# Summing half of the power tables by accumulating transfers, and turning the first batch's rows on TensorE

## The reference

```python
h = tok(x, log_dt, log_w_real, w_imag)      # (8, 256, 512)
#   dt = exp(log_dt); w = -exp(log_w_real) + i*w_imag; dtA = w*dt       (256, 64)
#   Cm = Cc * (exp(dtA) - 1) / w;  K = einsum('chn,hnl->chl', Cm, exp(dtA * arange(512)));  h = 2*K.real
h = concatenate([h, txt], axis=1)           # (8, 384, 512)
h = h + attn(layernorm(h))                  # compress to 64, layernorm, q/k/v, rope, causal softmax, out
h = h + ffn(layernorm(h))                   # shared expert + top 2 of 8 routed experts, hidden 352
```

## Time and profile before

| | |
|---|---|
| median of 3 runs | 830.52 us |
| profiled execution, its own time | 835.92 us |
| its span, first to last instruction | 834.1 us |
| TensorE busy | 758.9 us, 91% |
| VectorE, ScalarE, GpSimd busy | 489.1, 310.3, 346.4 us |
| mean granted TensorE clock | 0.973 |

### The profile page before, as it was taken

The page is one execution under the profiler, slowest core; times in us unless marked ns, Lnnn a source line. Parts: engine busy times, 40 slices in busy tenths (PEclk is TensorE's granted clock), DMA queues, the critical chain, the costliest instruction groups (busy, mean ns, idle before and its releaser), DMA issues.

```text
span 834.1 us, 19002 instructions
## 1 busy us (share of the span) xinstructions
PE 758.9 (91%) x6723; PEld 474.8 (57%) x6724; DVE 489.1 (59%) x922; ACT 310.3 (37%) x600; POOL 346.4 (42%) x362
## 2 busy tenths in 40 slices
PE   0099998989889999999999989999999999999985
PEld 0099996645455454564555535656656565666652
DVE  7987658387884766657954524554444444444442
ACT  6767425144224261544423403333232322323221
POOL 2278651151480030400067743545455554455433
PEclk9999997679999999999999999999999999999998
DMA  5342171035345051777353457978768777676753
GB/s 219 71 134 80 42 248 52 22 101 127 70 137 103 27 153 53 186 204 171 97 140 86 129 119 180 174 136 137 149 121 139 132 136 137 133 143 123 122 98 52
DMA packets 127534, 101.84 MB, mean 122 GB/s; under 512 B 96016, under 2 KB 96144, under 8 KB 126960
## 3 DMA queue, kind: packets, MB, share of 16 engines
q1 hardware_dynamic: 99984, 45.74, 23.8%
q0 software_dynamic: 14240, 30.06, 19.9%
q10 hardware_dynamic: 13248, 25.17, 10.8%
HBM read 48.46 MB, written 28.15 MB: 92 GB/s over the span
## 4 chain that ended last, share of the span: by engine, by line
PE 75%; DVE 9%; DMA 6%; POOL 4%; issue 3%; ACT 2%; SPq 0%; POOLq 0%; DVEq 0%; ACTq 0%
PE PS L2213 11%; PE PS L2215 11%; PE PS L2214 11%; PE PS L1159 9%; PE PS L1160 9%; PE PS L1161 9%; PE PS L662 6%; PE PS L819 3%; DMA out_dram<-work 2%; PE PS L2236 2%; PE PS L1376 1%; DVE big L1519 1%; DVE work L1524 1%; POOL big L482 1%; DMA big<-x_dram,work 1%
## 5 line engine op out<-in xcount | busy, mean ns | idle before, releaser
L2213 PE MATMUL PS<-big,work 128*128 x493 | 165.8, 336 | 5.0 <-DMA work<-big 2.7
L2214 PE MATMUL PS<-big,work 128*128 x493 | 165.7, 336 | 0.0
L2215 PE MATMUL PS<-big,work 128*128 x493 | 165.7, 336 | 0.0
L2385 POOL DMA_INDIRECT out_dram<-work x55 | 88.1, 1602 | 115.5 <-DMA out_dram<-work 62.3
L2278 ACT ACTIVATE work<-PS 128x768 f16<-128x768 f16 x55 | 44.6, 810 | 163.9 <-PE PS L2236 163.9
L2327 DVE SCALAR_TENSOR_TENSOR work<-work 128x352 f16<-128x352 f32 x55 | 32.2, 586 | 89.6 <-ACT work L2285 89.6
L1768 POOL DMA_INDIRECT slots_dram<-work x48 | 48.9, 1019 | 79.8 <-DVE work L2129 61.4
L2369 POOL DMA_INDIRECT big<-x_dram,work x55 | 55.3, 1005 | 46.3 <-POOL work L2366 46.3
L2213 PEld LDWEIGHTS PS<-big,work 128*128 128x128 f16 x493 | 48.5, 98 | 39.8 <-issue 6.2
L2215 PEld LDWEIGHTS PS<-big,work 128*128 128x128 f16 x493 | 48.4, 98 | 36.3
L2214 PEld LDWEIGHTS PS<-big,work 128*128 128x128 f16 x493 | 48.4, 98 | 33.6
(11 more groups left out here) (282 smaller groups left out, 1628.1 us busy)
## 6 DMA issues: line engine op xcount, KB each, us to landing
big<-in_weights ACTq DMA_DIRECT2D x33, 272.0 KB, 3.9
work<-in_weights ACTq DMA_DIRECT2D x31, 272.0 KB, 3.1
work<-in_shared ACTq DMA_DIRECT2D x28, 256.0 KB, 3.2
x_dram<-big SPq DMA_DIRECT2D x24, 256.0 KB, 2.3
out_dram<-big SPq DMA_DIRECT2D x24, 256.0 KB, 2.4
big<-big SPq DMA_DIRECT2D x4, 384.0 KB, 4.7
big<-in_par SPq DMA_DIRECT2D x1, 1185.0 KB, 10.5
big<-in_c_real SPq DMA_DIRECT2D x1, 1024.0 KB, 5.6
```

The costliest lines, as they stand in the source:

```text
L2213: pe.matmul(out, x_high, w_high, start=start, stop=False)
L2214: pe.matmul(out, x_high, w_low, start=False, stop=False)
L2215: return pe.matmul(out, x_low, w_high, start=False, stop=stop)
L2385: pool.indirect_dma_start(out_d, bass.IndirectOffsetOnAxis(ap=S_NUM[u][:, 0:1], axis=0), YO[u], None, compute_op=ALU.add).then_inc(s_add[u ...
```

## The change

In the token stage the b half of chunks 1 to 7 gets its power tables PB1 and PB2 in three rotating buffers; DVE builds both, and a transfer issued by POOL adds PB2 to PB1 in SBUF. TensorE then runs two products instead of four in that half. The a half keeps four products, its P2 built by POOL (by DVE in chunk 1). The first five weight pieces for the norms come by one transfer at the start. In the attention part the third compression is split in three, the fourth comes ahead of `q_tensor(1)`, and the three row tiles of batch 0 are turned by TensorE from XS in SBUF, their remainders taken by DVE; the scores of pair 1 move behind the first FFN unit. The DRAM store of these rows stays, their turned load goes. `bias(1)` moves to the front of POOL's list, splits of the pieces 2 to 10 move to other places, and ACT runs one small Exp ahead of `copy_compressed(0)`.

```diff
+        def summed(n):
+            return 16 * (n // 3 + (n % 3 > 0))
 # tok_sync
+            sp.dma_start(NORM_IN..., a["shared"][:, 0:EARLY_NORMS * SP_COLS]).then_inc(s_norms, 16)
 # tok_scalar, tables(n): waits for G1_{n-2}b; wi for every chunk (b half only from chunk 2), im with both groups from chunk 2
+            act.wait_ge(s_norms, 16)
+            for q in range(3):
+                square_norm(act, q)
             tables(0)
...
-                for q in range(2 * n, min(2 * n + 2, MCH)):
-                    square_norm(act, q)
+                    if x == 0 and EARLY_NORMS + n < MCH:
+                        square_norm(act, EARLY_NORMS + n)
 # tok_gpsimd
+            def sum_b(n):
+                pool.wait_ge(tok_v.sem, tok_v.at(f"P2_{n}b"))
+                pool.dma_start(PB1[n % 3], PB2[n % 3], accum_op=ALU.add).then_inc(s_sum[n % 3], 16)
+            g2(0, "a")
+            g2(0, "b")
+            for n in CHUNKS[1:]:
+                if n not in VECTOR_P2:          # VECTOR_P2 = (1,)
+                    p2(n)                       # a half; waits im_n and mm{n-2}a
+                g2(n, "a")
+                if n >= 4:
+                    sum_b(n)
+                g2(n, "b")
+                if n < 4:
+                    sum_b(n)
 # tok_vector
+            def powers_b(n):
+                if n >= 3:
+                    dve.wait_ge(tok_p.sem, tok_p.at(f"mm{n - 3}b"))
+                p1(n, "b", grid(PB1[n % 3]))
+                p2(n, "b", grid(PB2[n % 3]))
+            for k in "ab":
+                p1(0, k, ...); p2(0, k, ...); g1(0, k)
+            powers_b(1)
+            for n in CHUNKS[1:]:
+                if n >= 2:
+                    dve.wait_ge(tok_p.sem, tok_p.at(f"mm{n - 2}a"))
+                p1(n, "a", ...)
+                if n in VECTOR_P2:
+                    p2(n, "a", ...)
+                g1(n, "a")
+                if n + 1 < NCHUNK:
+                    powers_b(n + 1)
+                g1(n, "b")
 # tok_tensor
+                    if n and x:
+                        pe.wait_ge(s_sum[n % 3], summed(n))
+                    products = [(power, coeff[u][...]) for power in (powers_of[:1] if n and x else powers_of) for coeff in (G1, G2)]
 # new functions of the attention part
+        def first_low(dve, t):
+            dve.wait_ge(lg_high, t + 1)
+            nc.vector.tensor_tensor(XS[t][:, D:2 * D], RX[t], XS[t][:, 0:D], ALU.subtract).then_inc(lg_low, 1)
+        def first_turn(pe):                     # 24 f16 transposes into banks 4, 5, 6
+            for part in range(2):
+                for t in range(3):
+                    if part == 0:
+                        pe.wait_ge(cm_a.sem, cm_a.at(f"cn{2 if t < 2 else 3}"))
+                    pe.wait_ge((lg_high, lg_low)[part], t + 1)
+                    for c in range(KC): mm = pe.transpose(...)
+        def first_columns(act): ...             # ACT copies t0 whole and the high half of t2 to XT_SH[0]
+        def first_rows(dve): ...                # DVE copies t1 whole and the low half of t2
 # attn_tensor
-            turn_probs(pe, 0, 0)
-            out_weights(pe)
-            turn_probs(pe, 0, 1)
             pe.wait_ge(tr_v.sem, tr_v.at(f"bank{2 * B - 4}"))
             pe.wait_ge(tr_a.sem, tr_a.at(f"bank{2 * B - 3}"))
-            compress(pe, 2)
+            compress(pe, 2, (0,))
+            turn_probs(pe, 0, 0)
+            turn_probs(pe, 0, 1)
+            out_weights(pe)
             values_tensor(pe, 0)
-            out_tensor(pe, 0)
-            q_tensor(pe, 1)
+            compress(pe, 2, (1,))
+            out_tensor(pe, 0, (0, 1))
+            compress(pe, 2, (2,))
+            out_tensor(pe, 0, (2,))
             compress(pe, 3)
+            q_tensor(pe, 1)
+            first_turn(pe)
             qkv_tensor(pe, 1)
-            scores_tensor(pe, 1)
-            pe.wait_ge(s_xt[0], 3 * 16)
+            turned_in(pe, 0)
             logits(pe, 0, XT_SH[0])
-            ffn_tensor(pe, 0, 4)
+            ffn_tensor(pe, 0, 1)
+            scores_tensor(pe, 1)
+            ffn_tensor(pe, 1, 4)
 # attn_vector (from the outputs of pair 0 on)
             scale_c(dve, 1, 1, 2)
+            out_stats(dve, 0, 0)
+            out_stats(dve, 0, 1)
             for w in OUT_ORDER[4:6]:
                 out_add(dve, 0, w)
+            out_stats(dve, 0, 2)
             moments(dve, 0, "a")
+            split_low(dve, 8)
+            norm_row(dve, 0); norm_row(dve, 1); first_low(dve, 0)
+            norm_row(dve, 2); first_low(dve, 1); first_low(dve, 2)
             for w in range(3, 6):
                 out_stats(dve, 0, w)
             moments(dve, 0, "b")
+            first_rows(dve)
+            rope_vector(dve, 1)
 # attn_gpsimd
+            bias(pool, 1)
             c_scale(pool, 1, 1, 2)
 # attn_scalar
+            act.activation(RSUM[:, 0, 0:1], lc("ones")[:, 0:1], ACT.Exp)
             copy_compressed(act, 0)
...
             exp_scalar(act, 0)
+            probs_scalar(act, 0, 0)
             copy_turned(act, 15)
             probs_scalar(act, 0, 1)
+            splits(act, 7, 8)                   # its load_piece(10) waits for split_low(6)
             ... WO copy
 # attn_sync
             store_rows(0)
-            sp.wait_ge(cm_p.sem, cm_p.at(f"c{PAIRS - 1}"))
-            load_turned(0)
```

More of the change, by code:

```diff
@@ L230, in build @@
         assert Q == HC * PW
+        HQ, PB_AT = Q // 2, 528
+        PB1, PB2 = ([x[u][:, HQ:Q] for u in range(2)] + [cut(work, PB_AT + k * HQ, HQ)] for k, x in enumerate((P1, P2)))
+        EARLY_NORMS = 5
+        NORM_IN = cut(big, Q, EARLY_NORMS, SP_COLS)
+        assert EARLY_NORMS * SP_COLS <= 2 * Q
         s_early, s_dt, s_w, s_c, s_late, s_par, s_rope, s_gate = (
@@ L389, in tables @@
                     act.wait_ge(set_v.sem, set_v.at("mag"))
[L390 to L394, removed]
+                at = 0 if n == 0 or n in VECTOR_P2 else HC * 4
+                for half in range(2):
+                    last = act.activation(bank(WI_BANK[n % 2], half, 1)[:, :, at:], turned(ROT, n, 1, 1, 2)[:, :, at:], ACT.Copy, scale=(1.0, -1.0)[half])
+                last.then_inc(tok_t.now(f"wi_{n}"), 1)
+                groups = 1 if n == 0 or n in VECTOR_P2 else 2
                 for half in range(2):
                     last = act.activation(turned(IM_ZW, n, half, 0, groups), turned(ROT, n, 1, 0, groups), ACT.Copy, scale=(1.0, -1.0)[half])
-                last.then_inc(tok_t.now(("zi" if n % 2 == 0 else "im") + f"_{n}"), 1)
+                last.then_inc(tok_t.now(f"im_{n}"), 1)
+            act.wait_ge(s_norms, 16)
+            for q in range(3):
+                square_norm(act, q)
             act.wait_ge(set_v.sem, set_v.at("mag_first"))
@@ L467, in tok_gpsimd, with part @@
                 pool.tensor_tensor(b1, b1, MAG_B[:, :, h0:h1].rearrange("p a h -> p h a"), ALU.mult).then_inc(set_g.now("mag2" + "ab"[x]), 1)
-            for n in CHUNKS:
-                u = n % 2
-                if n >= 2:
[L471 to L481, removed]
-                    pool.tensor_tensor(grid(G2[u])[:, h0:h1], slow(V, n, h0, h1), fast(ZI, n, h0, h1), ALU.mult).then_inc(tok_g.now(f"G2_{n}{k}"), 1)
+            def part(x, n, k):
+                return grid(x[n % 2])[:, HALVES[k]]
@@ L1743, in attn_gpsimd @@
                     deviation(pool, i, "ab"[half])
-                    rows_low(pool, 6 * i + 3 * half)
-                    if i == 0 and half == 0:
-                        bias(pool, 1)
+                    if i or half:
+                        rows_low(pool, 6 * i + 3 * half)
                     if i == 1 and half == 1:
@@ L1823, in attn_scalar @@
             copy_turned(act, 7)
[L1824 removed]
+            splits(act, 5, 6)
             v_scalar(act, 0)
```

225 lines of the change are left out of this document (139 added, 86 removed).

## The result

The changed kernel takes 818.78 us against 830.52 for the kernel before, medians of five runs each; the ratio, estimated from the runs and not from the two medians, is 0.9877, 95% interval 0.9833 to 0.992. The forecast was 808 in a range of 798 to 825: the sign is right, the gain is about half of what was forecast. A further measurement of the same kernel, six runs against 23 of before, gave 818.43 against 827.53, ratio 0.9866 (0.9808 to 0.9923).

A forecast was written before the change was run, and what follows sets the result against it. TensorE was taken to bound the kernel from 240 us on, unchanged, with gains only ahead of that: token stage -10.3, scores to logits -17.0, later waits +5, sum -22.3 us; 808 us against the median 830.52, range 798 to 825.

The forecast's parts named there:

- 17.0 us: Scores of pair 0 to first logits and half a unit beyond: gain of 17.0 us, bounds 20 and 7.
- Token stage, -10.3 forecast: Token stage: fewer TensorE products, POOL slowest at 6.5 us a chunk, end at 98.1 instead of 108.4 us.
- rival C: Token stage: the 3 us pause for sum 3 brings the clock down until compression 1 ends; 837 us, chance 0.07.
- Rival B: Token stage: sum slow to land or issue, TensorE waits in every b part; 816 to 818, up to 828; chance 0.15.
- From token stage to logits, 51.4 forecast: End of token stage to first logits: 51 us instead of 69.5, with no window at half clock.
- the split of piece 7 ahead of WO costs nothing: Before the WO copy: outputs free at 142.4 us, TensorE comes at 143.0, so the moved split costs nothing.
- I charge nothing: POOL's bias of pair 1, moved to DVE's statistics (136 to 144 us): no cost, 2.5 us at the upper bound.
- rival A: Second stretch, before the logits: the clock falls again, price 0.48 x 20.9 = 10 us; 818 us, chance 0.15.
- q, k, v as what is late next: Ahead of the first logits: q, k, v run until about 159.8 us, after the turned rows are copied by 159.3.
- A wait of 1.8 us ahead of unit 3: First FFN units: unit 3 needs the bank of unit 0, whose Silu is late on ACT; new wait of 1.8 us.
- The +5 for 200 to 240 us: After the logits: TensorE meets DVE's unchanged chores sooner and waits about 5 us more, bounds 0 and 10.
- rival D: Before 240 us: DVE and ACT absorb the second stretch's gain, 12 us lost; 820 us, chance 0.07.

The follow-up runs named there:

- the quick execution: One execution of the kernel before, unchanged, the same as h2; 826.85 us, nearest to the median.
- f4: The whole change with each sum issued as two transfers of half the columns; 817.03 us, ratio 0.9894 to the kernel before.
- f3: The whole change with a plain copy of PB2 over PB1 instead of the accumulating transfer; 816.45 us, ratio 0.9875 to the kernel before.
- the filled kernels: The kernel before with idle products in TensorE's two pauses of over 2.5 us: 20 and 18 of them, 828.4 us; 11 in each, 827.45 us.
- forecast's: The profiled execution of the kernel before, unchanged, from which the prediction was read; 835.92 us.
- f1: The kernel before, unchanged, executed once more for a second profile; 832.54 us.
- h2: The kernel before, unchanged, one execution; 826.85 us.
- h3: The kernel before, unchanged, one more execution; 828.78 us.

## Why the prediction was wrong in size

The step that failed is the last one, 808 = 830.52 - 22.3: it takes from the median a gain that was read from an execution which the median is not like. Two terms were too large besides. By its own steps, against the quick execution at the first FFN sum: -22.3 forecast, + 8.0 (clock) + 4.1 (token stage, 10.3 less 6.2) + 4.4 (to the logits, 69.5 less 51.4 forecast and 68.9 less 55.2 measured) - 2.7 (behind the logits, +6.1 forecast, +3.4 measured) = -8.5, as measured there.

- **The frame: the step that failed, 8.0 us.** To subtract from the median what the profile would gain holds only if the profile is like the median in the stage that changes. The text knew 5.4 us between the two and took the gain from the stretch where they were. Of its 17.0 us, 8.0 were recovered clock that an execution near the median had never lost (178.0 against 170.0). Profile against profile the change does show 17.2 of the 22.3 us.
- **Token stage, -10.3 forecast, -6.2 measured.** The landing (6.0 forecast, 5.1 to 6.9 with a median of 5.6), the issue (0.8; records of 0.85 to 1.77, but the next operation starts 0.6 later) and POOL's halves (1.9) were right. The pause of 3 us for sum 3 was 0.6, so rival C, the slower side, had no ground; where such a pause did come, 3.54 us in f4, the half clock behind it lasted 6.8 us and not 37. Wrong was what else those transfers touch: TensorE's instruction loads, 4.9 us of "issue" and then one short stretch at half clock, as far as the dates tell. The prediction had no term for it. Rival B looked for a late landing or issue; the sum is neither. The row that was set against 3.2 us for a plain copy, 4.1 for 256 KB, is of a transfer to DRAM; plain copies in SBUF took 3.4 in f3. (The prediction's dates have 86.3 where 67.0 and three times 6.5 give 86.5, which changes nothing.)
- **From token stage to logits, 51.4 forecast, 55.2 measured.** The forecast counts from the end of TensorE's last half chunk; counted from the copy's end, as the 55.2 are, it is 50.8. f4, whose clock stays up, needs 52.9, 2.1 more, of which the wait for the WO copy can explain 1.8; the other 2.3 us, up to 55.2, come with the clock. That the split of piece 7 ahead of WO costs nothing failed together with "I charge nothing" for the bias: neither brings the wait without the other. The rows showed the contention for tables of 384 columns, and it was looked for at the remainders, which ran undisturbed; it struck at operations of 6 columns, at 0.65 to 0.84 us more each, where DVE's split, ACT's load and the WO copy hang on one another. The fall of the clock behind it is rival A at a third of its price (0.48 x 6.8 us, 3.3), in this execution. The Trainium skill (SBUF — State Buffer, Who interferes with whom) has a VectorE instruction with two SBUF inputs contend with a GpSimd one that reads SBUF; these rows agree, 0.80 to 1.01 us beside POOL's bias and 0.15 to 0.17 without it.
- **q, k, v as what is late next** was right: with the wait taken off, the rows' chain (1.41 us) and q, k, v bound it at 52.7, within 1.9 us of the 50.8.
- **A wait of 1.8 us ahead of unit 3**: 2.08 measured. **The +5 for 200 to 240 us** was too much: from the logits to the first FFN sum the change is 3.4 us slower, and about 4 are the moved scores and this wait, already in the 17.0. What the 5 stood for, DVE holding TensorE up, is there on both sides: 2.62 us of wait at the sums of pair 1 in the quick execution, 2.81 in the change. Where it grows, in the filled kernels, it is rival D in small.
- **No change behind that point**: 607.9 against 608.2 us, right.

The chances gave 0.86 to faster, and faster it was. The value, 818.8, lies in the range and on the 818 of rivals A and B, each of which had 0.15, but that is luck: what happened is a piece of A, a cost beside B, and the frame, which no rival named.

None of the variants is shown to be faster than the whole change: even without the transfers the median is 816.2. What a cheaper sum would bring stays open. With the plain copy Y is complete 6 us earlier, the medians differ by 2 us, and the interval of its four runs is 6 us to either side.

## What to carry to other kernels

Before a forecast is set against the median, compare the profile's mean clock with that of the other runs: where a stage holds a stretch at half clock and the profile is one of the long executions, price that stage a second time at full clock. The sums here cost more than their landing (0.6 us of waiting for them, 4.9 of "issue"): ask what else the DMA engines carry at that time, the engines' instructions included. And when an operation is costed at nothing because another is short, check that other for a neighbour that may stretch it.

## What the hardware showed beyond that

- The same pause of 2.61 us, behind the same instructions, was followed by a granted clock of 0.50 for 23.9, 17.1, 3.4 and 3.4 us in four executions of one kernel (forecast's, f1, h2, h3). What decides between them stays open; the price was up to 9 us of 830. The wait of 1.8 us in the changed kernels varies likewise: 6.8 us at 0.50 right behind it, or none.
- An accumulating transfer of 512 KB in SBUF lands in 5.6 us (5.1 to 6.9) where a plain one takes 3.4 (2.9 to 4.9). The Trainium skill (DMA: Bandwidth & Descriptors, Anatomy of one DMA — SWDGE (gpsimd) path) fits one transfer by 2.0 us and 436 GB/s, 3.2 us for 512 KB, and doesn't say for which kind: the plain copies agree with it, the sums don't.
- TensorE stood still for 2.25 us with all operands ready, while a packet of the "instruction" queue started only at the end of another queue's packets; the profile books it as "issue".
- While POOL added tables of 512 columns, operations of DVE on 6 columns took up to 1.01 us instead of 0.17.
